# The router's one-hot rows, written for eight places by one instruction, with the partition's factor on ScalarE

## The reference

```python
logits = jnp.einsum('sbd,de->sbe', x, Wg) + bg + bias
vals, idx = jax.lax.top_k(logits, TOP_K)                      # TOP_K = 2 of 16
w = jax.nn.softmax(vals - jnp.max(vals, axis=-1, keepdims=True), axis=-1)
cw = jnp.einsum('sbk,sbke->sbe', w, jax.nn.one_hot(idx, NUM_EXPERTS, dtype=x.dtype))
h = jax.nn.relu(jnp.einsum('sbd,edh->esbh', x, W1) + b1[:, None, None, :])
y = jnp.einsum('esbh,ehd->esbd', h, W2) + b2[:, None, None, :]
out = jnp.einsum('esbd,sbe->sbd', y, cw)
```

## Time and profile before

| | |
|---|---|
| median of three runs | 1701.73 us (1700.77 to 1705.13) |
| the profiled execution | 1696.73 us |
| its span in the trace | 1695.0 us |
| the router's block | 1260.4 to about 1349 us of the span |
| the one-hot stretch in it | 1312.17 to 1346.61 us |
| VectorE busy over the span | 1181.9 us (70%) |
| TensorE busy over the span | 1505.3 us (89%) |

### The profile page before, as it was taken

The page is one execution under the profiler, slowest core; times in us unless marked ns, Lnnn a source line. Parts: engine busy times, 40 slices in busy tenths (PEclk is TensorE's granted clock), DMA queues, the critical chain, the costliest instruction groups (busy, mean ns, idle before and its releaser), DMA issues. The chain is left out here.

```text
span 1695.0 us, 40131 instructions
## 1 busy us (share of the span) xinstructions
PE 1505.3 (89%) x14096; PEld 987.2 (58%) x14097; DVE 1181.9 (70%) x2272; ACT 983.3 (58%) x2029; POOL 429.5 (25%) x702
## 2 busy tenths in 40 slices
PE   6999999999999999998999956998774599999990
PEld 5843333333333333335788856887662299999990
DVE  7689999999999999943788676454568822222225
ACT  3428888888888888882555413343222055555543
POOL 3045401111010101001022237221221145555540
PEclk9968999999999999999999958898887599999995
DMA  6950232323332323002000003233119432222218
GB/s 217 296 158 17 46 60 50 61 52 65 53 63 47 69 49 59 9 22 34 1 1 0 1 15 101 56 101 102 51 36 325 155 108 71 71 68 71 71 59 300
DMA packets 117062, 135.24 MB, mean 80 GB/s; under 512 B 29540, under 2 KB 85880, under 8 KB 116792
## 3 DMA queue, kind: packets, MB, share of 16 engines
q1 hardware_dynamic: 104152, 107.60, 25.0%
q0 software_dynamic: 7584, 20.72, 3.8%
q10 hardware_dynamic: 5184, 4.98, 0.9%
HBM read 92.23 MB, written 36.04 MB: 76 GB/s over the span
## 5 line engine op out<-in xcount | busy, mean ns | idle before, releaser
L2007 DVE TENSOR_REDUCE mx<-ps 128x1 f32<-128x1024 f32 x512 | 622.7, 1221 | 21.6 <-PE ps L2156 16.2
L2045 ACT ACTIVATE PR<-ps 128x512 f32<-128x512 f32 x1024 | 557.2, 599 | 83.8 <-PE ps L2210 28.1
L2156 PE MATMUL ps<-KQ 48*128 48x512 f32 x1024 | 387.2, 460 | 4.0 <-DVE mx L2007 3.6
L2210 PE MATMUL ps<-KQ 50*128 50x512 f32 x1024 | 377.9, 449 | 0.1
L2192 PE MATMUL ps<-PR,VO 128*32 128x256 f32 x4096 | 328.9, 393 | 9.2 <-ACT PR L2045 8.7
L2210 PEld LDWEIGHTS ps<-KQ 50*128 50x128 f32 x1024 | 154.4, 186 | 215.8 <-ACT PR L2045 198.4
L2192 PEld LDWEIGHTS ps<-PR,VO 128*32 128x32 f32 x4096 | 80.7, 108 | 195.1 <-ACT PR L2045 99.4
L2156 PEld LDWEIGHTS ps<-KQ 48*128 48x128 f32 x1024 | 158.1, 191 | 21.3 <-DVE mx L2007 20.7
L1899 PEld LDWEIGHTS ps<-e_xinT,e_w 128*128 128x128 f32 x1264 | 155.0, 193 | 5.8 <-issue 1.9
L1899 PE MATMUL ps<-e_xinT,e_w 128*128 128x128 f32 x1264 | 155.7, 277 | 1.1 <-ACT e_xinT L1813 1.1
L1889 PE MATMUL ps<-eW,e_hiddenT 128*128 x632 | 149.3, 379 | 0.0
(11 more groups left out here) (288 smaller groups left out, 2160.4 us busy)
## 6 DMA issues: line engine op xcount, KB each, us to landing
qk_parts<-parts SPq DMA_DIRECT2D x8, 2048.0 KB, 8.5
TB<-toeplitz_lines SPq DMA_DIRECT2D x32, 512.0 KB, 6.5
KQ<-qk_parts SPq DMA_DIRECT2D x96, 128.0 KB, 4.6
KQ<-qk_parts SPq DMA_DIRECT2D x192, 64.0 KB, 2.4
eW<-in_L_ffn_W SPq DMA_DIRECT2D x16, 512.0 KB, 6.6
eW<-in_L_ffn_W SPq DMA_DIRECT2D x8, 1024.0 KB, 12.6
e_got<-expert_outputs SPq DMA_DIRECT2D x16, 512.0 KB, 8.2
X<-in_L_attn_x SPq DMA_DIRECT2D x8, 512.0 KB, 4.3
```

What stands on the lines that cost most here:

```text
L2007: nc.vector.tensor_reduce(mx[:, u % RING, h * QT + q:h * QT + q + 1], ps[:, b:b + 2].rearrange("p a n -> p (a n)"), AX, ALU.max, negate=Tr ...
L2045: nc.scalar.activation(PR[:, kt % 2, h], ps[:, st_bank(u, s)], ACT.Exp).then_inc(exp_done, 1)
L2156: made = nc.tensor.matmul(ps[:, max_bank(u, t) + k], of_tile(queries(u % RING), h, q), kq[half(h, KROWS), 0, h % HR, k * BANK:(k + 1) * BA ...
L2210: nc.tensor.matmul(ps[:, st_bank(u, s)], kq[half(h, AROWS), 0, h % HR, kt * P:(kt + 1) * P], queries(u % RING)[half(h, AROWS), qc, h % HR] ...
```

## The change

The three rows of a place are no longer written one place at a time with the choice's tile or row as a per-partition scalar. For a whole block of eight places VectorE now issues three two-operand instructions (`tensor_tensor`), in which the choice's tile or row is a second operand that is repeated along the row: `same_tile`, one at the choice's tile and zero elsewhere (8 x 80 = 640 elements); `in_lane` (8 x 128 = 1024); and `in_tile[.., 1]`, `same_tile` times the place's slot number (640). `in_tile[.., 0]` is `same_tile` times the partition's number, and ScalarE makes it, by one activation per block. `same_tile` lies in the memory of `xT`, which is free by then. The slot numbers come from a new table `slot_no`: one more `iota` on GpSimd and one more conversion on VectorE. TensorE's eight matmuls of a block wait for all of the block's rows at once.

```diff
+            same_tile = xT[:].rearrange("p h k n -> p (h k n)").bitcast(BF16)[:, 0:2 * PLACES * MTP].rearrange("p (s j m) -> p s j m", s=2, j=PLACES)
+            si, slot_no = sbuf(s0, "r_si", [P, 2 * NT], I32), sbuf(s0, "r_slot_no", [P, 2 * NT])
...
                     nc.gpsimd.iota(pi[:], pattern=[[1, 1]], base=0, channel_multiplier=1).then_inc(iotas, 1)
+                    nc.gpsimd.iota(si[:], pattern=[[1, 2 * NT]], base=FREE, channel_multiplier=0).then_inc(iotas, 1)
...
-                    dve.wait_ge(iotas, 5)
-                    for dst, src in ((lane, ai), (tile_no, ti), (part_no, pi), (own, oi)):
+                    dve.wait_ge(iotas, 6)
+                    for dst, src in ((lane, ai), (tile_no, ti), (part_no, pi), (own, oi), (slot_no, si)):
...
                     def rows(n, s, i):
+                        over = lambda v, w: v.unsqueeze(2).broadcast_to([P, PLACES, w])
+                        each = lambda v, w: v.unsqueeze(1).broadcast_to([P, PLACES, w])
+                        tile, row = (at2[:, a, s, i:i + PLACES] for a in range(2))
                         dve.wait_ge(summed, n + 1)
-                        for j in range(PLACES):
-                            tile, row = (at2[:, a, s, i + j:i + j + 1] for a in range(2))
-                            nc.vector.tensor_scalar(in_tile[:, s, j, 0], tile_no[:], tile, part_no[:], ALU.is_equal, ALU.mult).then_inc(one_hot, 1)
-                            nc.vector.tensor_scalar(in_tile[:, s, j, 1], tile_no[:], tile, float(FREE + NT * s + i + j), ALU.is_equal, ALU.mult).then_inc(one_hot, 1)
-                            nc.vector.tensor_scalar(in_lane[:, s, j], lane[:], row, None, ALU.is_equal).then_inc(one_hot, 1)
+                        nc.vector.tensor_tensor(same_tile[:, s], each(tile_no[:], MTP), over(tile, MTP), op=ALU.is_equal).then_inc(tiles_known, 1)
+                        nc.vector.tensor_tensor(in_lane[:, s], each(lane[:], P), over(row, P), op=ALU.is_equal).then_inc(lanes_known, 1)
+                        dve.wait_ge(tiles_known, n + 1)
+                        slots = slot_no[:, NT * s + i:NT * s + i + PLACES]
+                        nc.vector.tensor_tensor(in_tile[:, s, :, 1], same_tile[:, s], over(slots, MTP), op=ALU.mult).then_inc(slots_known, 1)
                     places(rows)
...
+                    def parts(n, s, i):
+                        act.wait_ge(summed, n + 1)
+                        act.wait_ge(tiles_known, n + 1)
+                        nc.scalar.activation(in_tile[:, s, :, 0], same_tile[:, s], ACT.Copy, scale=part_no[:]).then_inc(parts_known, 1)
+                    places(parts)
...
                     def add(n, s, i):
+                        pe.wait_ge(lanes_known, n + 1)
+                        pe.wait_ge(parts_known, n + 1)
+                        pe.wait_ge(slots_known, n + 1)
                         for j in range(PLACES):
-                            pe.wait_ge(one_hot, 3 * (PLACES * n + j + 1))
```

More of the change, by code:

```diff
@@ L1518, in moe @@
             lt_done, lt_kept, wg_zeroed, owners_known = sem("r_lt_done"), sem("r_lt_kept"), sem("r_wg_zeroed"), sem("r_owners_known")
-            hot_ready, gap_ready, one_hot, summed = (sem("r_" + n) for n in ("hot_ready", "gap_ready", "one_hot", "summed"))
+            hot_ready, gap_ready, lanes_known, tiles_known, slots_known, parts_known, summed = (
+                sem("r_" + n) for n in ("hot_ready", "gap_ready", "lanes_known", "tiles_known", "slots_known", "parts_known", "summed"))
             stored = [sem(f"r_stored{h}") for h in range(2)]
```

## The result

The kernel takes **1690.1 us** (median of 17 runs, 1683.3 to 1699.3) against 1701.9 before (17 runs, 1697.5 to 1720.5). The ratio is 0.9923, with a 95% interval of 0.9901 to 0.9945: 9 to 17 us less. The prediction was 1689.5 us, 12.2 less.

A forecast was written before the change was run, and what follows sets the result against it. VectorE's writing of one-hot rows was taken to lie on the path; its gain of 12.64 us less 0.47 for the last burst made 12.2 us, so 1701.73 would become 1689.5 us, range 1683 to 1696.

The forecast's parts named there:

- VectorE's gain, 12.64 us: Router's one-hot stretch: 24 grouped instructions take VectorE 20.93 us where 192 single ones took 33.57.
- The last burst, 0.47 us: End of the one-hot stretch: VectorE waits 1.34 us for the last eight matmuls, 0.87 before; costs 0.47, up to 1.7.
- ScalarE's 0.85 us: One-hot blocks: ScalarE's activation of 640 elements takes 0.85 us, covered by VectorE's two later instructions with 1 us to spare.
- point (d): One-hot blocks: slot rows or ScalarE wait; an activation over 1.8 us would show, 3 us costing 10 us; 2 in 100.
- (a): Grouped one-hot rows: repeated float operand beside a bf16 one halves VectorE's rate; kernel 7.0 us slower, 1708.7; 4 in 100.
- (b): Grouped one-hot rows: VectorE runs them at bf16's double rate; 9.6 us more off, 1680; 4 in 100.
- The trade of rate for fixed parts: VectorE's one-hot rows: the lost element rate costs 15 us, 168 fixed parts taken away are worth 27 us.
- Ahead of the stretch: Before the one-hot rows: the added iota and conversion fall into idle time and cost nothing; without cover 0.45 us.
- (c): Expert tiles: TensorE's clock rise shifts, 2.5 us further off to 5 us on; over 5 us of clock shift, 6 in 100.
- the same 1312 us: Sign in the new profile: the first two-operand one-hot row starts at 1312 us, as the first one-hot row did before.
- the first fetch at 1337.3: Sign in the new profile: GpSimd's first fetch, after the reading of the sum, comes at about 1337.3, before at 1349.49.
- The median: Whole kernel: median of three runs before, 1701.73 us, less 12.2 gives 1689.5 us.

The follow-up runs named there:

- x_places4: Changed kernel with four places to a block in place of eight; stretch from first one-hot row to reading of the sum 23.53 us, changed 22.41.
- x_tiles_only: Changed kernel with the lane rows written one place at a time again, tile rows still grouped; one-hot stretch 23.73 us, changed 22.41.
- x_lanes_only: Changed kernel with both tile rows written one place at a time on VectorE, only lane rows grouped, nothing on ScalarE; one-hot stretch 33.73 us, changed 22.41.
- x_scalar_x3: Changed kernel with ScalarE's activation done three times per block, TensorE waiting for all; one-hot stretch 22.86 us, changed 22.41.
- x_scalar_x4: Changed kernel with ScalarE's activation done four times per block, TensorE waiting for all; one-hot stretch 25.49 us, changed 22.41.
- x_bf16_operand: Changed kernel with the repeated operands (tile, row and slot number) held in bf16 in place of float; one-hot stretch 22.41 us, as changed.
- x_pair_inner: Changed kernel with pairs of places innermost in both matmul operands, TensorE's step two elements; one-hot stretch 12.60 us, kernel 1681.2 us, ratio to before 0.9860.
- x_tile_inner: Changed kernel with eight places innermost in the streamed tile rows only, tile, row and slot number in bf16; one-hot stretch 20.90 us, changed 22.41.

## Why the prediction was right, step by step

- **VectorE's gain, 12.64 us.** Right to the hundredth: from the first row to the end of the last 1339.76 - 1318.82 = 20.94 us, forecast 20.93. The durations 0.82 and 1.22 us were those read off L1608 and L1960 (forecast 0.825 and 1.225), and the overlap of 0.09 us read off L1614 held. x_places4 shows the fixed part at another size, x_tiles_only and x_lanes_only the old instructions'.
- **The last burst, 0.47 us.** The mechanism and the burst (1.22 us, forecast 1.24) were right; the cost is 0.60 us. From the end of the last row to the reading it is 1.47 us (1.34 forecast, 0.87 before), since the burst starts 0.14 us behind the slot rows and L1673 starts 0.11 us behind the burst, not 0.05 each. L1667 to L1671 fill 0.83 us of it, so VectorE waits 0.64, where 0.4 to 0.5 was named as the sign. Gain less cost is 12.63 - 0.60 = 12.03 us.
- **ScalarE's 0.85 us.** 0.83, with a microsecond to spare. But point (d) was wrong: it said that an activation of over 1.8 us would show in each block. x_scalar_x3 (2.3 us, stretch +0.45, all of it behind the last block) refutes it. The step that failed is the one that took one block alone: TensorE's wait for ScalarE matters to VectorE only two blocks later, so what is compared is ScalarE's time per block with VectorE's, 2.6 us, and x_scalar_x4 shows the pace set by ScalarE beyond it. The forecast did not hang on it.
- **Rate (a) and (b).** (a) fell with the first L1660 of 1.22 us. (b) fell too. Against it the prediction had the float operands, and the repetition within the row, which no row of before showed for bf16; x_bf16_operand shows that the repetition is enough by itself. Float operands without a repetition were not tried.
- **The trade of rate for fixed parts.** The reckoning that 168 fixed parts are worth more than the lost rate held (27 against 15 us). But nearly all of it lies in the two tile rows of 80 (11.3 us, of which 2.4 are ScalarE's) and hardly any in the lane rows of 128 (1.3 us).
- **Ahead of the stretch and the clock (c).** The iota and the conversion left no trace that could be told from the 11 us by which the stretch's start scatters; so the stretch did not start at the same 1312 us, which the prediction had named as a sign, nor the first fetch at 1337.3 (it came at 1344.12). Behind the stretch the profiled executions differ by 0.7 us, within the scatter of 3.2. In the expert tiles TensorE's granted clock reads 0.50 until 1358 before and until 1352 after, 5.3 and 4.7 us behind the first transposes: no shift of the size that (c) asked for.
- **The median.** 1701.86 x 0.9923 = 1688.8 by the ratio and 1690.1 by the median, forecast 1689.5. That close an agreement is partly luck: the interval of the ratio is 7.5 us wide.

## What to carry to other kernels

Count a row of small VectorE instructions by what lies from start to start, and weigh the fixed part against the elements: here a row of 80 elements cost 0.15 to 0.22 us at the fast rate, of which 0.02 were elements, and one instruction for eight rows won in spite of a rate of a quarter. When an operand must be repeated, put the index over which it is not repeated innermost, in runs of two if another engine reads the result, and look at that engine's step. Behind two buffers an engine has a whole block of time, here between 2.3 us, which only the last burst felt, and 2.9, which every block felt. And a stage's gain is to be measured in the stage when the whole scatters by as much.

## What was not expected of the hardware

- TensorE streams bf16 with a step of eight elements at 0.289 us for 160 columns, with a step of one or two at 0.133, at half clock; the same step in the loaded weights leaves the pace as it is (1.26 us a burst against 1.22). The Trainium skill has SBUF lines of 16 bytes and full rate only with two hits or more to a line (SBUF — State Buffer, the note on cachelines): a step of 16 bytes hits each line once, one of 4 bytes four times, and the trace agrees on both for the streamed operand. The same note also gives eight bf16 elements as the distance one can stride for free; here a step of eight costs a factor of 2.2 on TensorE, and the measurement decides. Steps between two and eight were not tried.
- VectorE holds the double rate of two-byte tensors with an innermost run of two elements: 0.684 us for 1024 where a repeated element gives 1.215.
- In x_pair_inner TensorE's clock rose within the one-hot stretch, which it did in none of the other twelve kernels: the last two bursts take 0.73 us in place of 1.22, the blocks being 1.41 or 1.49 us apart and TensorE working for 1.2 of each until then. It reads 0.50 again from 1336 on, TensorE having been idle since 1332. Fewer gaps alone do not explain the rise: in x_tile_inner the profile has TensorE busy without a gap, with matmuls slowed by the step of eight, and the clock stays at 0.50. Why it rises in the one and not in the other is open. First x_pair_inner at the first burst at full clock, then x_tile_inner (busy by engine, PEclk, DMA share, GB/s):

```profile
1329.00:1330.00 1.00, 0.51 (x8) 0.33 (x6) 1.00 (x3) 0.62 (x1) 0.00 (x0) 1.00 1.10 347
```
```profile
1316.00:1331.00 15.00, 15.00 (x54) 5.82 (x52) 12.95 (x22) 4.97 (x6) 0.00 (x0) 0.50 0.98 311
```
